# Attention and two expert layers on one core: value tiles padded with zeros, roots taken in groups, input rows added by transfers, earlier loads between phases, and the reciprocal on GpSimd

## The chip, the core and the metric

The kernel runs on one core of a Trainium2 chip. Its time is the device time of one execution in microseconds; the execution that the profiler recorded is one more. TensorE (PE; its weight loads are PEld) multiplies matrices into PSUM, VectorE is DVE, ScalarE is ACT, GpSimd is POOL, and SP only issues transfers. Each engine works through its own list of instructions in order and waits on semaphores.

## The reference

Two layers over 4096 tokens of width 256, all in float32, each closed by a layer norm:

```python
h = x + attention(rmsnorm(x, s1))             # 16 heads of 16, chunks of 64 tokens
h = h + moe(rmsnorm(h, s2))                   # 8 experts, top 2, capacity 1280, gelu, hidden 1024
x = layernorm(x + h)
x = layernorm(x + ffn(x))                     # layernorm inside, 8 experts, top 2, silu(g) * u, capacity 1280
```

The attention is linear. With phi(y) = elu(y) + 1, q and k rotated (rope) and then put through phi, v plain and g a sigmoid gate, each chunk first adds itself to the state and then reads it:

```python
S = S + einsum('bhtd,bhte->bhde', kc, vc)
Z = Z + kc.sum(axis=2)
num = einsum('bhtd,bhde->bhte', qc, S)
den = einsum('bhtd,bhd->bht', qc, Z)[..., None] + 1e-06
out = gc * (num / den)
```

The experts take the first 1280 tokens that chose them; their outputs, scaled by the gates, are added to the token's row.

## The kernel before

There are six phases, each a block in which every engine has its list, and between which all engines meet: `attention_phase`, `routing_phase`, `expert_phase` (E1), `between_phase` (norm, second router, second routing), `expert_phase` (E2), `final_phase` (norm and store).

**Attention** goes over 32 tiles of 128 tokens. `run_tiles` calls `step(t, at)` on every engine; in it `at(d)` is tile t + d, so one step holds work on several tiles: tile t+1 is projected and rotated, tile t updates the state and reads it, tile t-1 is gated and goes through the output projection, tile t-2 is normed and stored. The order on each engine is the order of the `if` blocks in its `step`. The pieces that the change touches, by the profile's lines:

- The values (L409, DVE) are written to `va`, 128 rows; the two chunks of the tile are its upper and lower 64 rows, and `add_chunk` (L459, PE) multiplies the 64 rows of one chunk with those of the keys into the state `b_s`, where 8 more columns of ones give Z. Masks (L384, DVE) copy the state after each chunk. L537 multiplies it by q: the state product.
- den is the last 8 columns per half of that product plus 1e-6 (L389, DVE), `rden` its reciprocal (L392, DVE, 128x16), `gr` gate times rden (L264, POOL), `og` is num times gr (L425, DVE). L522 transposes og, L345 copies it, L544 multiplies it by Wo. The gate is tanh with an affine step (L332, L336, ACT).
- x1 is the output of attention plus the input and bias (L400, DVE, from xb, L287, POOL). X += x1 (L270, POOL) is stored as the accumulator `acc1` (SP), and the normed x1 as `xn1`.
- The two rms norms take a mean square (ACT) to the power -0.5 on POOL, one column for each tile: r1 (L295) and r2 (L283).
- Rope needs rb (L279, POOL, two halves), ra (L437) and their sum rot (L445) on DVE; then ex (L361, ACT) and phi (L406, DVE).
- In the 16 steps of `W_STEPS` ACT and POOL also split a part of the first expert's weights (L357, L300).

Ahead of the steps, DVE scales all attention weights by the norm's scale (L370, L371), ACT and DVE split them into a high and a low part (L307, L374), and `extend_weights` (L475 to L484, PE) folds Wo and the router. DVE waits for all small loads at once.

**The seams.** At the end of an expert phase GpSimd waits for its last scatter into `acc1` or `acc2` (`pool.wait_ge(s_ys, ...)`), then all engines meet. The next phase loads the accumulator into X in eight groups of four tiles (L1108, L1256) and works group by group. To fill TensorE's time, `keep_busy` (L1061) runs matmuls whose result nobody reads: 46 at the end of E1, 12 ahead of the second router, and one for each tile there.

## Time and profile before

| | us |
|---|---|
| median of 3 runs | 1609.31 |
| lowest and highest | 1609.05, 1611.48 |
| the profiled execution | 1607.13 |
| its span | 1605.2 |

| engine | busy, share of the span |
|---|---|
| PE | 93% |
| PEld | 89% |
| DVE | 64% |
| POOL | 49% |
| ACT | 45% |

The span runs from the first to the last instruction recorded. Attention ends at about 253 us, the first routing at 288, E1 at 777, the second norm and routing at 852, and E2 at 1571. The row PEclk of the profile shows TensorE's granted clock in tenths of full speed.

### The profile page before, as it was taken

The page shows a single profiled execution, that of the slowest core. Times are in us where ns is not written, and L with a number is a line of the kernel's source. Part 1 is how long each engine was busy: PE and PEld are TensorE (multiplying, and loading weights), DVE is VectorE, ACT ScalarE, POOL GpSimd, SP SyncE. Part 2 cuts the span into 40 slices and gives each one's busy share as a digit, 9 for nine tenths or more (in the row PEclk, how much of TensorE's full clock was granted, in tenths as well). Part 3 has the DMA queues.
Part 4 walks back from the last instruction along what each step waited for, and adds up shares of the span by engine and source line. Part 5 has one row for each costly group of instructions (what it writes and reads, how often), then busy time and mean ns, then how long its engine had stood idle before and what let it go on. Part 6 is the DMA issues. An engine that isn't in the chain of part 4 may idle for free. (4 is left out here: it accounts for less than half of the span.)

```text
span 1605.2 us, 36263 instructions
## 1 busy us (share of the span) xinstructions
PE 1491.0 (93%) x11777; PEld 1435.2 (89%) x11777; DVE 1025.9 (64%) x2891; ACT 729.9 (45%) x1737; POOL 790.6 (49%) x799
## 2 busy tenths in 40 slices
PE   5999995799999999999967999999999999999990
PEld 4877774799999999999866999999999999999990
DVE  4888887567667667667374556565655656565553
ACT  3666554445455455555353434344343434343324
POOL 3899981456666566664322443444344344334420
PEclk9999996799999999999976999999999999999995
DMA  7111110333433343352412141323132132312216
GB/s 245 38 37 41 41 41 20 112 95 46 100 92 49 95 96 54 87 128 37 144 80 102 27 115 30 105 33 108 30 75 66 30 105 33 112 27 31 35 15 216
DMA packets 63829, 119.28 MB, mean 74 GB/s; under 512 B 14481, under 2 KB 52881, under 8 KB 61585
## 3 DMA queue, kind: packets, MB, share of 16 engines
q0 software_dynamic: 35840, 42.38, 16.1%
q1 hardware_dynamic: 27920, 76.07, 13.1%
q8 instruction: 32, 0.52, 0.1%
q14 instruction: 37, 0.30, 0.1%
HBM read 79.71 MB, written 38.71 MB: 74 GB/s over the span
## 5 line engine op out<-in xcount | busy, mean ns | idle before, releaser
L841 POOL DMA_INDIRECT acc<-E_ysb,IDX x160 | 258.4, 1615 | 133.8 <-ACT E_ysb L931 65.3
L836 POOL DMA_INDIRECT E_mg<-meta,IDX x160 | 151.0, 944 | 336.1 <-DVE E_gate L952 310.2
L968 DVE TENSOR_TENSOR E_hraw<-E_sg,bank 128x256 f32<-128x256 f32 x320 | 134.6, 421 | 283.3 <-ACT E_sg L904 283.3
L1021 PE MATMUL bank<-E_xT,ws 128*128 128x256 f32 x960 | 271.5, 283 | 5.0 <-DVE E_xT L943 5.0
L1022 PE MATMUL bank<-E_xT,ws 128*128 128x256 f32 x960 | 271.0, 282 | 0.0
L1023 PE MATMUL bank<-E_xT,ws 128*128 128x256 f32 x960 | 270.7, 282 | 0.0
L979 DVE TENSOR_TENSOR E_hT<-E_hraw,E_hT 128x256 fp32r<-128x256 f32 x640 | 259.3, 415 | 0.0
L975 DVE CAST E_hT<-E_hraw 128x256 fp32r<-128x256 f32 x640 | 201.1, 314 | 60.0 <-ACT E_hraw L907 52.9
L904 ACT ACTIVATE E_sg<-bank 128x256 f32<-128x256 f32 x320 | 121.4, 384 | 253.1 <-PE bank L1023 251.4
L1021 PEld LDWEIGHTS bank<-E_xT,ws 128*128 128x128 f32 x960 | 182.5, 190 | 5.8 <-issue 5.8
L1021 PE MATMUL bank<-ws,E_hT 128*128 128x256 f32 x640 | 183.7, 287 | 0.0
L1022 PEld LDWEIGHTS bank<-E_xT,ws 128*128 128x128 f32 x960 | 182.6, 190 | 0.0
L1023 PEld LDWEIGHTS bank<-E_xT,ws 128*128 128x128 f32 x960 | 182.4, 190 | 0.0
L1023 PE MATMUL bank<-ws,E_hT 128*128 128x256 f32 x640 | 180.1, 281 | 0.0
L1022 PE MATMUL bank<-ws,E_hT 128*128 128x256 f32 x640 | 180.0, 281 | 0.0
L1021 PE MATMUL bank<-E_xT,ws1b 128*128 128x256 f32 x640 | 179.5, 280 | 0.0
L1022 PE MATMUL bank<-E_xT,ws1b 128*128 128x256 f32 x640 | 179.5, 280 | 0.0
L1023 PE MATMUL bank<-E_xT,ws1b 128*128 128x256 f32 x640 | 179.4, 280 | 0.0
L907 ACT ACTIVATE E_hraw<-bank,E_b 128x256 f32<-128x256 f32 x320 | 141.7, 474 | 48.6 <-PE bank L1023 40.6
L831 POOL DMA_INDIRECT E_xg<-acc,IDX x80 | 80.6, 1007 | 146.8 <-ACT E_xgn L886 101.8
L467 PE MATMUL bank<-A_wsp,A_xT 128*128 128x512 f32 (+2 forms) x576 | 119.7, 344 | 4.4 <-DVE A_xT L433 4.4
L831 POOL DMA_INDIRECT E_xg<-xn,IDX x80 | 82.1, 1026 | 83.6 <-PE bank L1014 39.0
(201 smaller groups left out, 3990.4 us busy)
## 6 DMA issues: line engine op xcount, KB each, us to landing
wraw<-in_w_ffn SPq DMA_DIRECT2D x8, 3072.0 KB, 10.4
wraw<-in_w_moe SPq DMA_DIRECT2D x8, 2048.0 KB, 8.0
X<-acc SPq DMA_DIRECT2D x16, 512.0 KB, 6.8
xn<-A_xn SPq DMA_DIRECT2D x32, 128.0 KB, 1.7
acc<-X SPq DMA_DIRECT2D x32, 128.0 KB, 1.8
acc<-X SPq DMA_DIRECT2D x8, 512.0 KB, 2.6
out<-C_xo SPq DMA_DIRECT2D x8, 512.0 KB, 2.8
X<-in_x SPq DMA_DIRECT2D x3, 1024.0 KB, 11.4
```

The lines of the kernel that those rows point to most:

```text
L467: ins = nc.tensor.matmul(out, xT[:, n % 2, a, k, :], wsp[:, b, k, cols], start=(k == 0 and m == 0), stop=(k == KD - 1 and m == 2))
L831: nc.gpsimd.indirect_dma_start(out=xg[:, j, :], out_offset=None, in_=row_dram, in_offset=at_slots(u, j)).then_inc(s_gx, 16)
L836: nc.gpsimd.indirect_dma_start(out=mg[:, j, :], out_offset=None, in_=meta_dram, in_offset=at_slots(u, j)).then_inc(s_gm, 16)
L841: nc.gpsimd.indirect_dma_start(out=acc_dram, out_offset=at_slots(u, j), in_=ysb[:, j, :], in_offset=None, compute_op=ALU.add).then_inc(s_y ...
L904: nc.scalar.activation(sg[:, f % RING, :], ps[:, 0:UW], ACT.Silu).then_inc(s_sg, 1)
L907: nc.scalar.activation(hraw[:, f % RING, :], ps[:, 0:UW], ACT.Gelu, bias=b1[:, bass.ds(e * NF + f, 1)]).then_inc(s_sg, 1)
L968: V.tensor_tensor(hraw[:, f % RING, :], sg[:, f % RING, :], bank[f % RING][:, UW:2 * UW], ALU.mult).then_inc(s_hm, 1)
L975: V.tensor_copy(hT[:, 0, f, :], hraw[:, f % RING, :]).then_inc(s_hh, 1)
L979: V.tensor_tensor(hT[:, 1, f, :], hraw[:, f % RING, :], hT[:, 0, f, :].bitcast(F32), ALU.subtract).then_inc(s_hl, 1)
L1021: nc.tensor.matmul(out, wh, mh, start=first, stop=False)
L1022: nc.tensor.matmul(out, wh, ml, start=False, stop=False)
L1023: return nc.tensor.matmul(out, wl, mh, start=False, stop=last)
```

## The change

It has these parts:

1. **Values padded with zeros.** `vf` (DVE) takes the values; ACT copies each chunk's 64 rows into a tile `vz` of its own, whose other 64 rows are zero. `add_chunk` multiplies all 128 rows.
2. **Reciprocal on GpSimd.** rden = den to the power -1, 128x16, on POOL. DVE forms `ng` = (tanh + 1) x num, POOL og = ng x rden; the factor 0.5 goes into Wo ahead of the steps. The affine step on ACT is gone.
3. **Grouped roots.** r1 is taken for 1, 3 and then 4 tiles at once, r2 for 2; the xn and logit rows follow in pairs. ACT sums the squares of the input five tiles ahead instead of three.
4. **Input rows by transfers.** SP stores x1 into acc1; POOL issues four transfers of 8 tiles (`add_plain`) that add X to it. E1 waits for them.
5. **Start.** Weights come in two halves, scaled while they are split; the first tile of X has its own transfer; TensorE runs 16 matmuls on zeros first, and the folding of Wo stands later.
6. **Early rows.** SP loads the first two groups of X inside the expert phase, when all scatters but the last unit's have landed (those tiles aren't in the last unit), and the other six in the next phase after the last has. GpSimd no longer waits, and blocks end without its drain. The fillers go from 46 to 26 and from 12 to 4.

The core of the diff:

```diff
+            pool.wait_ge(loads, 16 * 4)
+            nc.gpsimd.tensor_scalar(wo[:, :, 0:D], wo[:, :, 0:D], 0.5, 0.0, ALU.mult, ALU.add).then_inc(s_half, 1)
 ...
                 if (n := at(-1)) is not None:
+                    pool.wait_ge(s_den, n + 1)
+                    after(pool, s_og, n)
+                    nc.gpsimd.tensor_tensor(rden[:, :, :], den[:, :, :], less1[:, :].unsqueeze(2).to_broadcast([P, KD, HPH]),
+                                            ALU.pow).then_inc(s_rden, 1)
                     pool.wait_ge(s_rden, n + 1)
-                    pool.wait_ge(s_g, n + 1)
-                    nc.gpsimd.tensor_tensor(by_head(gr[:, n % 2, :]), by_head(gt[:, n % 2, :]),
+                    pool.wait_ge(s_ng, n + 1)
+                    nc.gpsimd.tensor_tensor(by_head(og[:, n % 2, :]), by_head(ng[:, :]),
                                             rden[:, :, :].rearrange("p k h -> p (k h)").unsqueeze(2).to_broadcast([P, H, DK]),
-                                            ALU.mult).then_inc(s_gr, 1)
-                if (n := at(-2)) is not None:
-                    nc.gpsimd.tensor_tensor(X[:, n, :], X[:, n, :], x1[:, n % 2, 0:D], ALU.add).then_inc(s_xacc, 1)
+                                            ALU.mult).then_inc(s_og, 1)
 ...
+                if t in (11, 19, 27):
+                    add_plain(nc, pool, io, X, kept, t // 8 - 1)
+def add_plain(nc, pool, io, X, kept, g):
+    t = slice(g * 8, (g + 1) * 8)
+    for b in range(2):
+        pool.wait_ge(kept[f"x1{b}"], 16 * (g + 1) * 4)
+    nc.gpsimd.dma_start(by_partition(io["acc1"])[:, t, :], X[:, t, :], accum_op=ALU.add).then_inc(kept["plus"], 16)
 ...
+                    for c in range(2):
+                        rows = slice(c * CHUNK, (c + 1) * CHUNK)
+                        nc.scalar.activation(vz[rows, n % 2, c, :, 0:P], vf[rows, :, :], ACT.Copy).then_inc(s_vz, 1)
 ...
-                    dve.wait_ge(s_den, n + 1)
-                    V.reciprocal(rden[:, :, :], den[:, :, :]).then_inc(s_rden, 1)
+                    dve.wait_ge(s_th, n + 1)
+                    V.scalar_tensor_tensor(out=ng[:, :].rearrange("p (k c) -> p k c", k=KD), in0=gt[:, n % 2, :].rearrange("p (k c) -> p k c", k=KD),
+                                           scalar=1.0, in1=num_ps[:, :, 0:P], op0=ALU.add, op1=ALU.mult).then_inc(s_ng, 1)
 ...
-                    ins = nc.tensor.matmul(s_ps[:, k, :], phi[rows, n % 2, D + k * P:D + (k + 1) * P],
-                                           va[rows, n % 2, k, :], start=False, stop=True, skip_group_check=True)
+                    ins = nc.tensor.matmul(s_ps[:, k, :], phi[:, n % 2, D + k * P:D + (k + 1) * P],
+                                           vz[:, n % 2, c, k, :], start=False, stop=True, skip_group_check=True)
 ...
+            sp.wait_ge(s_ys, 16 * UT * (UNITS - 1))
+            for g in range(HEAD):
+                t = slice(g * G, (g + 1) * G)
+                sp.dma_start(X[:, t, :], by_partition(acc_dram)[:, t, :]).then_inc(s_head[g], 16)
 ...
-            pool.wait_ge(s_ys, 16 * UT * UNITS)
-                keep_busy(nc, bank[7], ws[0], 46)
+                keep_busy(nc, bank[7], ws[0], 26)
 ...
-            for g in range(GROUPS):
+            sp.wait_ge(s_ys, 16 * UT * UNITS)
+            for g in range(HEAD, GROUPS):
 ...
-            keep_busy(nc, bank[7], ws0, 12)
+            keep_busy(nc, bank[7], ws0, 4)
```

GpSimd's list in one attention step with expert weights, before (A_r from A_ssq is a root, ws a part of the weights):

```order
L264 TENSOR_TENSOR A_gr<-A_gt,A_rden 128x256
L270 TENSOR_TENSOR X<-X,A_x 128x256
L279 TENSOR_TENSOR A_rb<-A_qk,A_rope 128x32x8 x2
L283 TENSOR_TENSOR A_r<-A_ssq,A_mhalf 128x1
L287 TENSOR_TENSOR A_xb<-X,A_bo 128x256
L291 TENSOR_TENSOR A_xb<-A_lx,A_bor 128x8
L295 TENSOR_TENSOR A_r<-A_ssq,A_mhalf 128x1
L300 TENSOR_TENSOR ws<-wraw,ws 128x256
```

and now:

```order
L288 TENSOR_TENSOR A_rden<-A_den,A_less 128x16
L293 TENSOR_TENSOR A_og<-A_ng,A_rden 128x256
L302 TENSOR_TENSOR A_rb<-A_qk,A_rope 128x32x8 x2
L306 TENSOR_TENSOR A_r<-A_ssq,A_mhalf 128x2
L310 TENSOR_TENSOR A_xb<-X,A_bo 128x256
L314 TENSOR_TENSOR A_xb<-A_lx,A_bor 128x8
L325 TENSOR_TENSOR ws<-wraw,ws 128x256
```

The addition into X is gone, a power of 16 elements has come ahead of og, and r2 comes for two tiles in every second step.

VectorE's list in one attention step, before, from og on:

```order
L425 TENSOR_TENSOR A_og<-bank,A_gr 128x256
L384 TENSOR_TENSOR A_sm<-bank,cst 128x272
L433 TENSOR_TENSOR A_xT<-bank,A_xT 128x256
L437 TENSOR_TENSOR A_ra<-A_qk,A_rope 128x512
L384 TENSOR_TENSOR A_sm<-bank,cst 128x272
L445 SCALAR_TENSOR_TENSOR A_rot<-A_ra,A_rb 128x512
L389 TENSOR_SCALAR A_den<-bank 128x16
L392 RECIPROCAL A_rden<-A_den 128x16
L400 TENSOR_TENSOR A_x<-bank,A_xb 128x264
L406 SCALAR_TENSOR_TENSOR A_phi<-A_ex,A_rot 128x512
L409 SCALAR_TENSOR_TENSOR A_va<-bank,A_r,A_bqkvg 128x2x128
L414 SCALAR_TENSOR_TENSOR A_gt<-bank,A_r,A_bqkvg 128x256
```

and now, from the first mask on:

```order
L446 TENSOR_TENSOR A_sm<-bank,cst 128x272
L423 TENSOR_TENSOR A_xT<-bank,A_xT 128x256
L446 TENSOR_TENSOR A_sm<-bank,cst 128x272
L496 TENSOR_TENSOR A_ra<-A_qk,A_rope 128x512
L501 SCALAR_TENSOR_TENSOR A_rot<-A_ra,A_rb 128x512
L505 SCALAR_TENSOR_TENSOR A_vf<-bank,A_r,A_bqkvg 128x256
L457 TENSOR_SCALAR A_den<-bank 128x16
L460 SCALAR_TENSOR_TENSOR A_ng<-A_gt,bank 128x256
L469 TENSOR_TENSOR x<-bank,A_xb 128x264
L475 SCALAR_TENSOR_TENSOR A_phi<-A_ex,A_rot 128x512
L479 SCALAR_TENSOR_TENSOR A_gt<-bank,A_r,A_bqkvg 128x256
L485 SCALAR_TENSOR_TENSOR A_qk<-bank,A_r,A_bqkvg 128x512
```

The reciprocal is gone, ng stands behind den, ra behind the second mask, and the values behind rot.

TensorE's list at the start, from tile 0's value projection on, before:

```order
L467 MATMUL bank<-A_wsp,A_xT 128x256 x6
L467 MATMUL bank<-A_wsp,A_xT 128x264 x6
L475 MATMUL bank<-cst,A_wo 128x128 x4
L481 MATMUL bank<-A_wqkvg,A_woT 128x8 x4
L484 MATMUL bank<-A_wqkvg,A_bob 128x8 x2
L467 MATMUL bank<-A_wsp,A_xT 128x512 x6
L501 MATMUL bank<-cst,X 128x128 x2
L507 MATMUL bank<-cst,A_phi 128x128 x2
L457 MATMUL bank<-A_zeros 128x272
L459 MATMUL bank<-A_va,A_phi 128x136 x2
```

and now:

```order
L528 MATMUL bank<-A_wsp,A_xT 128x264 x6
L543 MATMUL bank<-cst,A_wo 128x128 x4
L528 MATMUL bank<-A_wsp,A_xT 128x512 x6
L536 MATMUL bank<-cst,X 128x128 x2
L574 MATMUL bank<-cst,A_phi 128x128 x2
L518 MATMUL bank<-A_zeros 128x272
L520 MATMUL bank<-A_vz,A_phi 128x136 x2
L528 MATMUL bank<-A_wsp,A_xT 128x256 x6
L520 MATMUL bank<-A_vz,A_phi 128x136 x2
L528 MATMUL bank<-A_wsp,A_xT 128x264 x6
L551 MATMUL bank<-A_wrs,A_woT 128x8 x4
L554 MATMUL bank<-A_wrs,A_bob 128x8 x2
```

The products with the transposed Wo and the bias (L481 and L484 before, L551 and L554 now; the projections are L467 before, L528 now) have moved from ahead of tile 1's projection to behind tile 0's state update.

## Rows read from the trace of the kernel before

**Rows 1.** busy time by engine in two windows: attention, second expert phase (columns as named)
```profile
core 0: us, PE busy (x) PEld busy (x) DVE busy (x) ACT busy (x) POOL busy (x), PEclk, DMA share, GB/s
200.00:240.00 40.00, 39.92 (x258) 31.74 (x256) 33.91 (x76) 22.55 (x71) 33.02 (x46) 1.00 0.11 37
866.00:1566.00 700.00, 700.00 (x5906) 700.00 (x5906) 409.13 (x1144) 271.15 (x582) 272.99 (x230) 1.00 0.26 59
```

**Rows 2.** timeline of TensorE's weight loads in one attention step (start us, us, what)
```profile
212.30 1.34 PEld L467 LDWEIGHTS bank<-A_wsp,A_xT 128*128 128x128 f32 x6
214.44 0.53 PEld L459 LDWEIGHTS bank<-A_va,A_phi 64*128 64x128 f32 x4 [0.17 <-issue]
215.10 0.78 PEld L467 LDWEIGHTS bank<-A_wsp,A_xT 128*128 128x128 f32 x6
216.01 0.53 PEld L459 LDWEIGHTS bank<-A_va,A_phi 64*128 64x128 f32 x4
216.67 0.20 PEld L522 LDWEIGHTS bank<-cst,A_og 128*128 128x128 f32 x2
219.17 1.34 PEld L467 LDWEIGHTS bank<-A_wsp,A_xT 128*128 128x128 f32 x6
```

**Rows 3.** GpSimd's instructions by form, attention, 180 to 235 us
```profile
L279 POOL TENSOR_TENSOR A_rb<-A_qk,A_rope 128x256 f32<-128x256 f32 x16 | 11.3, 729 | 6.9 <-DVE A_qk L420 6.9
L270 POOL TENSOR_TENSOR X<-X,A_x 128x256 f32<-128x256 f32 x9 | 9.4, 1039 | 1.0 <-DVE A_x L400 0.5
L287 POOL TENSOR_TENSOR A_xb<-X,A_bo 128x256 f32<-128x256 f32 x8 | 9.3, 1162 | 0.0
L283 POOL TENSOR_TENSOR A_r<-A_ssq,A_mhalf 128x1 f32<-128x1 f32 x8 | 8.0, 1004 | 0.0
L264 POOL TENSOR_TENSOR A_gr<-A_gt,A_rden 128x256 f32<-128x256 f32 x8 | 5.0, 622 | 0.1
L295 POOL TENSOR_TENSOR A_r<-A_ssq,A_mhalf 128x1 f32<-128x1 f32 x7 | 3.8, 548 | 0.0
L291 POOL TENSOR_TENSOR A_xb<-A_lx,A_bor 128x8 f32<-128x8 f32 x8 | 1.6, 200 | 0.0
```

**Rows 4.** two of VectorE's by form, same stretch
```profile
L400 DVE TENSOR_TENSOR A_x<-bank,A_xb 128x264 f32<-128x264 f32 x8 | 3.5, 433 | 4.8 <-PE bank L544 4.8
L392 DVE RECIPROCAL A_rden<-A_den 128x16 f32<-128x16 f32 x8 | 2.0, 254 | 0.3
```

**Rows 5.** timeline of the start, VectorE and TensorE
```profile
14.09 0.48 DVE L377 TENSOR_SCALAR A_bob<-cst,A_bcol 128x128 f32<-128x128 f32 x2 [1.34 <-DMA A_bcol<-in_bcol]
...
31.33 0.69 PE L537 MATMUL bank<-A_sm,A_qT 128*64 128x136 f32 x8
```

**Rows 6.** timeline between attention and the first routing
```profile
252.49 0.29 ACT L351 ACTIVATE LG<-A_x,A_r 128x8 f32<-128x8 f32 x1
...
255.40 0.43 DVE L636 TENSOR_TENSOR LG<-LG,rbias 128x256 f32<-128x256 f32 x1 [4.74 <-PEq L116]
```

**Rows 7.** timeline between the first experts and the second routing
```profile
772.00 10.60 PE L1061 MATMUL bank<-ws 128*128 128x512 f32 x46
...
775.79 1.55 POOL L841 DMA_INDIRECT acc<-E_ysb,IDX  x1 [0.30 <-issue]
...
783.71 4.04 SPq L1108 DMA_DIRECT2D X<-acc  x8
...
785.58 4.58 PE L1061 MATMUL bank<-ws 128*128 128x512 f32 x12
790.00 0.38 PE L1210 MATMUL bank<-cst,X 128*128 128x128 f32 x2
```

**Rows 8.** timeline between the second experts and the final norm
```profile
1577.41 3.95 SPq L1256 DMA_DIRECT2D X<-acc  x8
1581.22 1.41 DVE L1298 BATCH_NORM_STATS2 C_st<-X 128x6 f32<-128x256 f32 x4 [18.41 <-DMA X<-acc]
...
1587.15 2.06 ACT L1274 ACTIVATE C_xo<-X,C_nb,C_rs 128x256 f32<-128x256 f32 x4
```

More of the change, by code:

```diff
@@ L36 @@
 UT = UW // P
+G = 4
+GROUPS = NT // G
+HEAD = (UPE - 1) * UW // (G * P)
 SC = E * TILES_E
@@ L93, in after @@
         eng.sem_inc(passed, 1)
-LEAD = 3
+LEAD = 5
 LAG = 2
+R1_GROUPS = [(0, 1), (1, 4)] + [(a, a + 4) for a in range(4, NT, 4)]
+X_SPANS = [(0, 1), (1, 4), (4, 8), (8, 16), (16, 24), (24, 32)]
 WX = 4 * D + E
@@ L104 @@
 W_STEPS = range(6, 22)
+WARM = 16
 WCHUNK = 4 * HID // len(W_STEPS)
@@ L219, in _ @@
             sp.dma_start(bo[:, :], io["bo"].partition_broadcast(P)).then_inc(loads, 16)
-            sp.dma_start(bcol[:, :], io["bcol"]).then_inc(loads, 16)
-            for g in range(1, 5):
+            sp.dma_start(cst[:, C_ID + P:C_N], io["consts"][:, C_ID + P:C_N]).then_inc(l_cst, 16)
+            for g in range(2, len(X_SPANS)):
                 rows_in(g)
@@ L304, in _, with high, turned @@
         def _(act):
-            for k in range(KD):
-                act.wait_ge(s_w, 2 * k + 2)
-                nc.scalar.activation(wsp[:, 0, k, :], wqkvg[:, k, :], ACT.Copy).then_inc(s_wh, 1)
+            def high(k, part):
+                nc.scalar.activation(wsp[:, 0, k, part], wqkvg[:, k, part], ACT.Copy, scale=cols[:, k:k + 1]).then_inc(s_wh, 1)
+            def turned(n):
+                act.wait_ge(s_tx, n + 1)
+                after(act, s_pjg, n - 1)
+                after(act, s_xl, n - 1)
+                nc.scalar.activation(xT[:, n % 2, 0, :, :], tx_ps, ACT.Copy).then_inc(s_xT, 1)
+            act.wait_ge(l_cols, 16)
+            act.wait_ge(l_wa, 16)
+            for k in range(KD):
+                high(k, half_a)
+            turned(0)
+            act.wait_ge(l_wb, 32)
+            for k in range(KD):
+                high(k, slice(2 * D, 4 * D))
+            act.wait_ge(s_wrs, KD)
+            for k in range(KD):
+                nc.scalar.activation(wsp[:, 0, k, 4 * D:WX], wrs[:, k, :], ACT.Copy).then_inc(s_wh, 1)
             def step(t, at):
@@ L450, in _ @@
         def _(pe):
-            pe.wait_ge(early, 16 * 5)
-            pe.wait_ge(s_cst, 4)
+            pe.wait_ge(s_cst, 1)
+            for _ in range(WARM):
+                nc.tensor.matmul(b_to[:, 0:KD * SW], zeros[:, 0:P], zeros[:, :], start=True, stop=True)
             def add_chunk(n, c):
-                rows = slice(c * CHUNK, (c + 1) * CHUNK)
                 if n % TPB == 0 and c == 0:
@@ L458, in add_chunk, with project, turn, turn_weights @@
                 for k in range(KD):
-                    ins = nc.tensor.matmul(s_ps[:, k, :], phi[rows, n % 2, D + k * P:D + (k + 1) * P],
-                                           va[rows, n % 2, k, :], start=False, stop=True, skip_group_check=True)
+                    ins = nc.tensor.matmul(s_ps[:, k, :], phi[:, n % 2, D + k * P:D + (k + 1) * P],
+                                           vz[:, n % 2, c, k, :], start=False, stop=True, skip_group_check=True)
                 ins.then_inc(s_sa, 1)
-            def project(n, out, cols):
+            def project(n, out, part):
                 for k in range(KD):
                     for m, (a, b) in enumerate(((0, 0), (0, 1), (1, 0))):
-                        ins = nc.tensor.matmul(out, xT[:, n % 2, a, k, :], wsp[:, b, k, cols],
+                        ins = nc.tensor.matmul(out, xT[:, n % 2, a, k, :], wsp[:, b, k, part],
                                                start=(k == 0 and m == 0), stop=(k == KD - 1 and m == 2))
                 return ins
-            def extend_weights():
-                pe.wait_ge(loads, 16 * 5)
+            def turn(n):
+                loaded(pe, n)
+                after(pe, s_xl, n)
+                for k in range(KD):
+                    ins = nc.tensor.transpose(tx_ps[:, k, :], X[:, n, k * P:(k + 1) * P], ident)
+                ins.then_inc(s_tx, 1)
+            def turn_weights():
+                pe.wait_ge(s_half, 1)
                 for m in range(KD):
@@ L495, in step @@
                     after(pe, s_qk, n)
-                    project(n, b_p0[:, :], slice(0, 2 * D)).then_inc(s_pj0, 1)
-                if (n := at(2)) is not None:
-                    loaded(pe, n)
-                    after(pe, s_xl, n)
-                    for k in range(KD):
-                        ins = nc.tensor.transpose(tx_ps[:, k, :], X[:, n, k * P:(k + 1) * P], ident)
-                    ins.then_inc(s_tx, 1)
+                    project(n, b_p0[:, :], half_a).then_inc(s_pj0, 1)
+                if (n := at(2)) is not None and n:
+                    turn(n)
                 if (n := at(0)) is not None:
@@ L846, in free_rows @@
                 pool.wait_ge(s_xgn if glu else s_tg, n * UT if glu else n)
+            if kept:
+                for b in range(2):
+                    pool.wait_ge(kept[f"xn{b}"], 16 * NT // 2)
             x_rows(0)
@@ L853, in _ @@
             meta_rows(1)
+            if kept:
+                pool.wait_ge(kept["plus"], 16 * NT // 8)
             for u in range(UNITS):
```

290 lines of the change are left out of this document (159 added, 131 removed).

## The prediction

> **What bounds the kernel now.** I read the stages first, as busy time in windows. The reader should see two kinds of stretch. In the second expert phase TensorE's weight loads fill 700.00 of 700 us at a granted clock of 1.00 [rows 1]; the change leaves the work inside both expert phases alone, so nothing moves there. In the attention phase, 40 us hold 39.92 us of matmuls but 31.74 us of weight loads, beside 33.91 us of VectorE and 33.02 us of GpSimd [rows 1]: three engines near the limit at once.
>
> So I read one attention step engine by engine. A step takes 219.17 - 212.30 = 6.87 us on TensorE, in which no wait for another engine stands, only gaps: 0.17 us ahead of the first state update (L459), 0.13 us behind it (215.10 - 214.97), 0.13 us ahead of the second (216.01 - 215.88) and 0.13 us behind it (216.67 - 216.54) [rows 2]. These are the places where the array goes from 128 rows to 64 and back. TensorE bounds the step. GpSimd idles there only for qk, 6.9 us in 8 steps, which is 0.86 us a step [rows 3]; VectorE idles 4.8 us for the output projection in 8 steps [rows 4], 0.6 us a step. A step shorter by more than about 0.9 us would meet one of the two.
>
> Last come the seams between phases: times at which one phase's last instruction and the next one's first stand apart [rows 5 to 8].
>
> **The state update on 128 rows.** Values go into a tile whose other half is zero, so L459's matmuls no longer use half of the array. The loads stay as many and as wide (4 in 0.53 us [rows 2]), so all there is to win is the four gaps, 0.56 us; they will not vanish wholly. I take 0.38 us a step, bounds 0 and 0.56. The price is two ScalarE copies of 64 partitions instead of the gate's affine step (L336), on an engine that waits several times a step for others: hidden, nothing. VectorE loses the reciprocal (0.254 us [rows 4]), and its og gives way to ng, as wide. Over 30 full steps: 30 x 0.38 = 11.4 us, if GpSimd keeps up.
>
> The Trainium skill, "TensorE: Matmul & The Clock Gate", Part 3, speaks against this edit: it says that a weight load runs under a matmul in flight only where the two use different row groups, an overlap which full-height matmuls give up. The trace shows no such overlap ahead of L459, but the gap of 0.17 us [rows 2]. By that rule alone this term would be 0 or a small loss; it is one of the rivals below.
>
> **GpSimd's step.** Removed: X += x1 (1.04 us), half of the r2 powers (1.00 each, beside a VectorE instruction), three of four r1 powers (0.55). gr (0.62) becomes og, of the same size. Added: rden as a power of 16 elements [rows 3]. What stays is 0.62 + 2 x 0.73 + 0.50 + 1.16 + 0.20 + about 0.15 = 4.1 us, and in the 16 steps that also split expert weights one more 256-wide instruction, 0.62: 4.7 us.
>
> What the power costs no row shows, since each power in this trace has one element. Below: 0.55 us, plus 15 elements at the rate of a plain operation, (0.622 - 0.200) / 248 = 0.0017 us each: 0.57 us. Above: a plain one-element operation is 0.19 us, so one power is 0.55 - 0.19 = 0.36 us more, and if each element pays that, it is 0.19 + 16 x 0.36 = 5.95 us. Which of the two the 0.36 us is, a preparation or a price per element, decides the case. I take 1.6 us, nearer to the one-element row than to the upper end. Then GpSimd needs 5.7 us a step, and 6.3 us in the steps with weights: under the 6.49 us of TensorE, by little. The Trainium skill, "GPSIMD Engine Reference", section 3.1, calls the operation a software loop over the elements in which the body is paid for each, and 4.1 advises against this engine for elementwise work. By it the upper bound is the likelier end; it is the first rival.
>
> The power adds a wait too, for den. og is wanted by the transpose L522, which stands 4.37 us into a step (216.67 - 212.30 [rows 2]), so for it a power of 3 us would still be in time. Behind the power on GpSimd are queued og and then rb, for which VectorE's rot waits. Before, X += x1 stood in that place and GpSimd then idled for qk, 1.04 + 0.86 us [rows 3]; only a power over 1.9 us makes rb late.
>
> **X plus x1 by transfers.** SP stores x1 instead of X, and four accumulating transfers of 1 MB add X later. A scatter of 128 rows takes GpSimd 1.55 us to issue [rows 7]; four issues, at most 6 us, in the idle time of the step. 0, bound 3 us. No wait is late by them: the only one who needs the sum is the first scatter, over 30 us on.
>
> **The start.** Before, VectorE passes its wait for all small loads at 14.09, and the first state product of tile 0 runs at 31.33 [rows 5]. In between lie the scaling of the weights and the folded router weights, which stood ahead of the second projection on TensorE. After, scaling is folded into the two splits, the weights come in halves, the roots of the first tiles are there early, and the folding stands behind the gate projection. What is loaded up to the last of the small loads falls from 3.1 to 2.7 MB, so they are in by about 14.09 x 2.7 / 3.1 = 12.3. An estimate of the chain from there, each instruction about 0.7 us and GpSimd's pair 1.5 [rows 3]: qk to 13.1, rb to 15, rot, ex and phi to 17.8, then gt, qk, two masks with TensorE between them, ra, rot, ex and the copies of the second round to about 24, the product at 24.5. That is 6.8 us earlier; the 16 warming matmuls on zeros may hold the first transpose, so I take 6.5, bounds 3 and 9.
>
> **The end of attention.** Before: the last router row at 252.49, the routing's first instruction at 255.40 [rows 6], 2.9 us, of which I take half as the wait for the last stores, which goes: 1.5 us. The last tile pays the power instead of 0.25 us, and the xn and logit rows of two tiles instead of one (about 0.8 us): -2.2 us. Sum -0.7.
>
> **First experts to the second routing.** Before, the last scatter is issued by 777.34, and everybody waits for it to land: the next phase begins at 783.71, and loads X, and TensorE turns the first tile at 790.00 after twelve filling matmuls [rows 7]. After, only SP waits for it; the phase opens at about 778.3, when GpSimd has issued and TensorE has run 26 instead of 46 fillers (46 took 10.60 us, so 26 end at 778.0 [rows 7]), and two of eight groups of X are there, loaded during the last unit. TensorE needs 785.58 - 783.71 = 1.87 us for the fold [rows 7] and 0.9 for four fillers: first turn at 781.1, which is 8.9 us earlier. When the scatter has landed no row shows; it is before 783.71, and I take 0.6 us before. The third group is there 3.8 us later (as a first group, 1581.22 - 1577.41 [rows 8]), at 786.9, about when the first eight tiles are turned. I take 8.5, bounds 5 and 10.
>
> **Second experts to the final norm.** Here ScalarE bounds the end, group behind group. The third group can't be loaded before the scatter has landed, again taken as 0.6 us before the opening, 1576.8, so it lands at 1580.6 and reaches ScalarE at 1583.0, with 2.4 us for its moments and root; before, the second group's rows started at 1587.15 [rows 8], and they come just ahead of it in the queue. So 4.1 us, bounds 3 and 7.
>
> **The sum.** 11.4 + 6.5 - 0.7 + 8.5 + 4.1 = 29.8 us. The profiled execution took 1607.1 us, its span 1605.2; it becomes 1577.3. The median of the runs is 2.2 us above it: 1579.
>
> **Rivals.**
> - *The power pays per element.* GpSimd becomes the bound of the attention step. With a power of p us the steps change by 14 x (p + 4.1 - 6.87) + 16 x (p + 4.7 - 6.87) = 30 p - 73.5 us, against 20 - p us won elsewhere. It decides from p = 3.0 us: there the change is worth nothing. At 4 us it is slower by 30 us (1640), at 5.95 by 91 us (1700). For it: 0.36 us for one element is much for mere preparation. Against it: a loop over independent elements may overlap them.
> - *Between the two*, 2.2 to 3.0 us: GpSimd eats the steps' gain and part of the rest, 1585 to 1609.
> - *The steps do not get shorter*, since the gaps stay, or VectorE's order (second mask, ra, rot, vf, den, ng, x1) closes a loop of the old length. All else holds: 1607.1 - 18.4, and with the median's offset 1591. For it: VectorE idles in only 0.9 us of a step, and TensorE's second update waits for its mask.
> - *The change does not do what it says* in the seams (the next phase still opens when the scatter has landed): 13 us less gain, 1592. SP is then the one that opens late; its order has the wait inside the next phase, so this is small.
>
> **Chances.** Forecast 0.48; the power per element, slower, 0.30; between 0.12; steps not shorter 0.07; seams 0.03. Within 0.2% (3.2 us, about what a measurement of this kernel tells from none) lies a sliver of the middle case: 0.04. Faster is 0.48 + 0.07 + 0.03 + 0.08 = 0.66, slower 0.30. The range reaches from 1570 (all terms at their good ends but one) to 1655 (a power of 4.5 us), which leaves out the highest powers; the forecast's own range is 1570 to 1592.
>
> **What the profile of the changed kernel would show.** The mean of the power of 16 elements on GpSimd: near 1.6 us, or several. The step on TensorE at 6.5 us, no gap beside the state updates, and no wait for og. GpSimd idle at rb for qk; if it never idles there, the first rival holds. The first state product near 24.5, TensorE's first turn of the second routing under 8 us behind the last expert matmul's 772, and the final phase opening under 6 us behind the last scatter's issue. I am wrong if the attention phase is longer than before.

## The result, and the profile after

The changed kernel takes 1618.2 us (median of 5 runs, 1617.6 to 1620.5), the kernel before 1609.3 us in runs on the same chip. The ratio is 1.0057, 95% interval 1.0041 to 1.0072: slower by 0.6%, where 1579 us were forecast. Its profiled execution took 1619.0 us, with a span of 1617.2 us, 12.0 more than before.

Where the 12.0 us come from, stretch by stretch. The attention steps are counted from the first instruction that writes the denominators (`A_den`) to the last, 31 intervals; "last scatter" is the start of its issue.

| Stretch | before | after | change | forecast |
|---|---|---|---|---|
| start to the first denominators | 32.1 | 26.8 | -5.3 | -6.5 |
| 31 attention steps | 213.5 | 243.5 | +30.0 | -11.4 |
| last denominators to routing | 9.9 | 11.1 | +1.2 | +0.7 |
| E1, last scatter to the first turned tile | 14.2 | 5.5 | -8.7 | -8.5 |
| E2, last scatter to the last output rows | 32.5 | 24.5 | -8.0 | -4.1 |
| all the rest: both routings, both expert phases, the last stores | | | +2.8 | 0 |

The four stretches at the start, the end of attention and the seams together won 20.8 us where 18.4 were forecast. The steps lost 41 us against the forecast. The windows show on which engine (columns: window, its length, then busy time with count for PE, PEld, DVE, ACT, POOL, then TensorE's granted clock, DMA share and GB/s):

```profile
60.00:200.00 140.00, 115.96 (x733) 93.73 (x732) 98.76 (x201) 77.01 (x249) 131.94 (x132) 0.96 0.19 49
200.00:240.00 40.00, 35.47 (x237) 29.13 (x238) 31.20 (x66) 22.32 (x74) 39.04 (x37) 1.00 0.09 31
```

Against [rows 1], TensorE falls from 39.92 to 35.47 us of 40, and GpSimd rises from 33.02 to 39.04: it hardly rests. Its instructions by form in the stretch of [rows 3] (busy us and mean ns of one, then the idle time ahead):

```profile
L288 POOL TENSOR_TENSOR A_rden<-A_den,A_less 128x16 f32<-128x16 f32 x7 | 21.1, 3009 | 0.5 <-DVE A_den L457 0.5
L302 POOL TENSOR_TENSOR A_rb<-A_qk,A_rope 128x256 f32<-128x256 f32 x14 | 11.7, 859 | 0.0
L310 POOL TENSOR_TENSOR A_xb<-X,A_bo 128x256 f32<-128x256 f32 x8 | 6.7, 837 | 0.0
L293 POOL TENSOR_TENSOR A_og<-A_ng,A_rden 128x256 f32<-128x256 f32 x7 | 4.8, 686 | 0.6
L306 POOL TENSOR_TENSOR A_r<-A_ssq,A_mhalf 128x2 f32<-128x2 f32 x4 | 2.8, 690 | 0.0
```

The 16-element power takes 3.0 us, not 1.6, and rb no longer waits for qk: the sign that the prediction gave for its first rival. By size it stands at the upper end of the prediction's middle case (2.2 to 3.0 us, 1585 to 1609); the kernel came out 9 us above that case. TensorE's loads show both the promised gain and the new wait:

```profile
200.01 0.20 PEld L574 LDWEIGHTS bank<-cst,A_phi 128*128 128x128 f32 x2 [1.20 <-DVE A_phi L475]
200.18 0.53 PEld L520 LDWEIGHTS bank<-A_vz,A_phi 128*128 128x128 f32 x4
200.64 0.78 PEld L528 LDWEIGHTS bank<-A_wsp,A_xT 128*128 128x128 f32 x6
201.52 0.53 PEld L520 LDWEIGHTS bank<-A_vz,A_phi 128*128 128x128 f32 x4
203.93 0.20 PEld L592 LDWEIGHTS bank<-cst,A_og 128*128 128x128 f32 x2 [1.88 <-POOL A_og L293]
```

The gaps of [rows 2] around the first state update are gone (200.18 follows 200.01, and 200.64 follows 200.18, without a pause); ahead of the second 0.10 us is left (201.42 to 201.52) of 0.13. But TensorE stands 1.20 us for phi and 1.88 us for og, which GpSimd hands over late. At the seams:

```profile
26.02 0.69 PE L611 MATMUL bank<-A_sm,A_qT 128*64 128x136 f32 x8 [1.79 <-issue]
...
280.23 0.28 ACT L388 ACTIVATE LG<-x,A_r 128x8 f32<-128x8 f32 x1
281.31 0.43 DVE L710 TENSOR_TENSOR LG<-LG,rbias 128x256 f32<-128x256 f32 x1 [3.44 <-PEq L130]
...
802.54 1.55 POOL L920 DMA_INDIRECT acc<-ysb,IDX  x1 [0.30 <-issue]
806.44 2.81 SPq L1188 DMA_DIRECT2D X<-acc  x6
808.08 0.38 PE L1290 MATMUL bank<-cst,X 128*128 128x128 f32 x2
...
1589.30 1.55 POOL L920 DMA_INDIRECT acc<-ysb,IDX  x1 [0.30 <-issue]
1592.82 2.97 SPq L1337 DMA_DIRECT2D X<-acc  x6
1596.83 1.41 DVE L1379 BATCH_NORM_STATS2 C_st<-X 128x6 f32<-128x256 f32 x4 [5.73 <-DMA X<-acc]
```

The first state product comes 5.3 us earlier than in [rows 5]. The wait of 2.9 us in [rows 6] is 1.1 us. The loads that need the scatter start 3.5 to 3.9 us behind the scatter's issue; before, 7.9 us in [rows 7] (783.71 - 775.79) and 8.0 at the last seam.

### The profile page after: what moved, and what is told of

The parts are those of the page before. It is cut to its first block and busy times, and to the rows that moved or that the text cites. A ratio compares the mean times of both kernels' runs of the same rounds, so it can differ in the third digit from the quotient of the medians.

```text
span 1617.2 us, 36347 instructions
## 1 busy us (share of the span) xinstructions
PE 1487.6 (92%) x11781; PEld 1436.5 (89%) x11781; DVE 1021.5 (63%) x2861; ACT 740.7 (46%) x1773; POOL 834.3 (52%) x767
## 5 line engine op out<-in xcount | busy, mean ns | idle before, releaser
L920 POOL DMA_INDIRECT acc<-ysb,IDX x160 | 258.2, 1614 | 134.7 <-ACT ysb L1014 66.0
L1106 PEld LDWEIGHTS bank<-ws,E_hT 128*128 128x128 f32 x640 | 121.0, 189 | 0.0
## 6 DMA issues: line engine op xcount, KB each, us to landing
wraw<-in_w_ffn SPq DMA_DIRECT2D x8, 3072.0 KB, 10.5
```

Of the source, the lines that this page charges most:

```text
L920: nc.gpsimd.indirect_dma_start(out=acc_dram, out_offset=at_slots(u, j), in_=ysb[:, j, :], in_offset=None, compute_op=ALU.add).then_inc(s_y ...
L1106: return nc.tensor.matmul(out, wl, mh, start=False, stop=last)
```

## The experiments

Each run's steps are the same 31 intervals, counted in its profiled execution. The ratios go by runs of the kernel before that were made beside each kernel; their medians were 1609.3 to 1611.9 us. In one table:

| Kernel | median us | ratio to before, 95% | 31 steps | us a step |
|---|---|---|---|---|
| before | 1609.3 | | 213.5 | 6.89 |
| changed | 1618.2 | 1.0041 to 1.0072 | 243.5 | 7.85 |
| e3: before + power | 1667.2 | 1.0315 to 1.0380 | 267.9 | 8.64 |
| e1: reciprocal on VectorE | 1590.5 | 0.9841 to 0.9903 | 218.4 | 7.04 |
| e2: half of it as a power | 1582.2 | 0.9792 to 0.9854 | 207.1 | 6.68 |
| e9: e1 + power nobody reads | 1580.0 | 0.9797 to 0.9829 | 206.7 | 6.67 |
| e14: e1, og behind qk | 1593.2 | 0.9867 to 0.9909 | 217.5 | 7.02 |
| e6: e1, roots tile by tile | 1589.4 | 0.9854 to 0.9896 | 215.9 | 6.96 |
| e15: e14 and e6, and final order | 1576.2 | 0.9763 to 0.9812 | 203.8 | 6.57 |
| e13: e2, roots tile by tile | 1587.8 | 0.9844 to 0.9877 | 212.8 | 6.86 |
| e5: changed, roots tile by tile | 1613.6 | 1.0017 to 1.0037 | 239.5 | 7.73 |
| e10: e2, updates on 64 rows | 1589.9 | 0.9865 to 0.9907 | 216.8 | 6.99 |
| e11: e2 with the drain | 1586.6 | 0.9843 to 0.9876 | 205.9 | 6.64 |
| e17: e2, no early rows | 1588.8 | 0.9838 to 0.9893 | 207.0 | 6.68 |
| e16: e14, no warming | 1592.3 | 0.9855 to 0.9910 | 217.7 | 7.02 |

Run e4, further down, is no version of the kernel and has no row. Kernels e2, e11 and e17 have the same steps, which shows how far 31 steps repeat: 205.9 to 207.1.

### What a power costs

> This kernel computes nothing of the reference: on 128 partitions GpSimd runs a power and a multiplication three times each at 1, 2, 4, 8, 16, 32 and 64 elements, nothing beside it, and then VectorE runs reciprocals of the same sizes. If a power is paid per element (theory), the means lie on a line: from the changed kernel's trace (548 ns for one element, 690 for two, 1007 for four, about 2.9 us for 16) near 0.39 + 0.156 us per element, so 5.4 us at 32 and 10.4 us at 64, while the multiplications stay near 0.2 to 0.3 us. If the 2.9 us were contention with the kernel's other engines (rival), 16 elements would take here what a preparation and a plain rate give, under 1 us.

Rows of four short windows, each holding one size:

```profile
L49 POOL TENSOR_TENSOR y<-x,h 128x1 f32<-128x1 f32 x3 | 1.7, 558 | 0.2
L49 POOL TENSOR_TENSOR y<-x,h 128x1 f32<-128x1 f32 x3 | 0.6, 190 | 0.2
...
L49 POOL TENSOR_TENSOR y<-x,h 128x16 f32<-128x16 f32 x3 | 8.7, 2896 | 0.2
...
L49 POOL TENSOR_TENSOR y<-x,h 128x64 f32<-128x64 f32 x1 | 10.5, 10527 | 0.1
```

The first row is the power of one element, the second the multiplication; the last two are powers. The power takes 558, 699, 1007, 1636, 2896, 5418 and 10,527 ns for 1 to 64 elements: a straight line of 0.38 us plus 0.158 us an element ((10.527 - 0.558) / 63). The theory holds; the rival falls, since nothing ran beside it. VectorE's reciprocal of 16 elements took 0.255 us here.

```diff
 # e3: before, in front of gr on GpSimd; the reciprocal on VectorE goes
+pool.wait_ge(s_den, n + 1)
+nc.gpsimd.tensor_tensor(rden, den, less1 (broadcast), ALU.pow).then_inc(s_rden, 1)
```

> The kernel before with one edit: the reciprocals as a 16-element power on GpSimd, ahead of gr. Theory (GpSimd's step is the sum of its instructions): it had 6.87 - 0.86 = 6.0 us of work a step, and 2.9 to 3.2 more make about 9.0, so 30 steps grow by 60 to 70 us: 1670 to 1680. Rival (only the wait for the denominators counts, and GpSimd's idle time takes most of the power): under 30 us longer, below 1640.

It is slower by 3.5%, and the rival falls: the steps grew by 54.4 us, from 213.5 to 267.9, a little under the theory's 60 to 70. The step is 8.64 us, not 9.0. The sum had taken the durations of the kernel before; with GpSimd as the bound some of its instructions are shorter:

```profile
L263 POOL TENSOR_TENSOR A_rden<-A_den,A_less 128x16 f32<-128x16 f32 x16 | 49.2, 3075 | 1.2 <-DVE A_den L394 1.2
L274 POOL TENSOR_TENSOR X<-X,A_x 128x256 f32<-128x256 f32 x16 | 11.7, 728 | 0.0
L287 POOL TENSOR_TENSOR A_r<-A_ssq,A_mhalf 128x1 f32<-128x1 f32 x16 | 9.6, 603 | 0.0
```

X += x1 is 0.73 instead of 1.04 us, and r2's power 0.60 instead of 1.00 [rows 3], while each half of rb is 0.92 instead of 0.73. The likely reason, which no run tests, is that they lie elsewhere beside VectorE's instructions. So in the kernel before the power alone costs 54 us of steps. The changed kernel's steps grew by 30 only; it had also taken X += x1 off GpSimd and grouped the roots.

### The power undone, and at the price that was assumed

```diff
 # e1: DVE, behind den
-(GpSimd) nc.gpsimd.tensor_tensor(rden, den, less1, ALU.pow).then_inc(s_rden, 1)
+V.reciprocal(rden[:, :, :], den[:, :, :]).then_inc(s_rden, 1)
 # e2: both engines, half each
+nc.gpsimd.tensor_tensor(rden[:, 0, :], den[:, 0, :], less1, ALU.pow).then_inc(s_rden, 1)
+V.reciprocal(rden[:, 1, :], den[:, 1, :]).then_inc(s_rdv, 1)
```

> The changed kernel with the reciprocal back on VectorE, all else kept. Theory: the 16-element power of 2.9 to 3.3 us alone makes the attention steps longer. GpSimd's step falls to 4.1 us (4.7 with weights), TensorE bounds it again, and the 31 intervals between the first and the last denominator take 202 to 214 us instead of 243.5; median 1578 (if the 128-row updates save 0.38 us a step) to 1589 (if they save nothing). Rival: the roots in pairs and the normalized rows of two tiles at a time, which tie ScalarE to GpSimd, make a good part of it: then the attention keeps over 225 us and the median is 1600 or more.

> The changed kernel, with the reciprocals of one half (8 elements) as a power on GpSimd and those of the other half on VectorE. By 0.39 + 0.156 us per element the power takes 1.64 us, the value that the prediction assumed for all 16, so this run measures whether the rest of the prediction's sum holds at that price: 1579 if its account of the step is right (GpSimd 5.7 us a step, 6.3 with weights, hidden under TensorE). Rival: a power of any such length is late for the two instructions behind it on GpSimd (the output copy and rb, for which VectorE waits), because it waits for the denominators first; then this is slower than the kernel with the reciprocal on VectorE by 10 us or more.

With the reciprocal on VectorE the kernel is 1.3% faster than the kernel before, so the power is the cause of the sign. But its steps, at 7.04 us, are longer than before, outside the 202 to 214 us that the theory gave and also far from its rival's 225. With half of the reciprocals, GpSimd's power is

```profile
L288 POOL TENSOR_TENSOR A_rden<-A_den,A_less 128x8 f32<-128x8 f32 x21 | 35.0, 1668 | 4.2 <-DVE A_den L458 4.2
```

1.67 us, the value assumed for all 16, and the median is 1582.2 against the 1579 forecast for that price. That the version with more work on GpSimd is faster by 8 us needed an explanation. VectorE's phi gives the lead, first e1, then e2 (60 to 200 us):

```profile
L473 DVE SCALAR_TENSOR_TENSOR A_phi<-A_ex,A_rot 128x512 f32<-128x512 f32 x20 | 20.6, 1031 | 0.0
```

```profile
L478 DVE SCALAR_TENSOR_TENSOR A_phi<-A_ex,A_rot 128x512 f32<-128x512 f32 x21 | 14.4, 684 | 0.0
```

The same instruction takes 1.03 us in the one and 0.68 in the other, with no wait ahead of it in either. The timeline of e1 says what lies beside it:

```profile
148.22 0.62 POOL L289 TENSOR_TENSOR A_og<-A_ng,A_rden 128x256 f32<-128x256 f32 x1
```

```profile
147.72 0.36 DVE L458 SCALAR_TENSOR_TENSOR A_ng<-A_gt,bank 128x256 f32<-128x256 f32 x1
148.00 0.42 DVE L467 TENSOR_TENSOR x<-bank,A_xb 128x264 f32<-128x264 f32 x1
148.33 1.05 DVE L473 SCALAR_TENSOR_TENSOR A_phi<-A_ex,A_rot 128x512 f32<-128x512 f32 x1
```

GpSimd's og starts as soon as ng is there, and so runs into phi. In e2 the power is beside phi, and og comes beside qk, which reads PSUM and keeps its 0.74 us (e2, GpSimd, then VectorE):

```profile
149.04 1.62 POOL L288 TENSOR_TENSOR A_rden<-A_den,A_less 128x8 f32<-128x8 f32 x1
150.74 0.62 POOL L294 TENSOR_TENSOR A_og<-A_ng,A_rden 128x256 f32<-128x256 f32 x1
```

```profile
149.38 0.68 DVE L478 SCALAR_TENSOR_TENSOR A_phi<-A_ex,A_rot 128x512 f32<-128x512 f32 x1
150.38 0.74 DVE L488 SCALAR_TENSOR_TENSOR A_qk<-bank,A_r,A_bqkvg 128x512 f32<-128x512 f32 x1
```

### Two locks on the step

A lock here is a wait or a slow instruction that holds the step's length by itself, so that removing another one shows nothing.

```diff
 # e9: all 16 reciprocals on VectorE; on GpSimd in the same place
+nc.gpsimd.tensor_tensor(unused[:, :], den[:, 0, :], less1, ALU.pow).then_inc(s_rden, 1)
```

> All 16 reciprocals on VectorE; GpSimd also takes a power of 8 elements at the same place, whose result nobody reads. The kernel with half of the reciprocals on GpSimd ran 8.2 us faster than the one with all on VectorE (1582.2 against 1590.5; 31 steps in 207.1 against 218.4 us), though it gives GpSimd 1.67 us more a step and takes only 0.05 us from VectorE's reciprocal. Theory: GpSimd's elementwise instructions slow VectorE's longest ones where the two lie side by side (phi 1.03 instead of 0.68 us), and the power, which does not, moves them away from phi. Then this kernel keeps phi near 0.68 us and takes 1582 to 1585. Rival: the 0.05 us of the shorter reciprocal stand on VectorE's chain, and with what hangs on them make the difference; then this is 1588 to 1592 with phi at 1.0 us.

The unused power alone brings 218.4 down to 206.7 us, with phi at 681 ns: the theory holds, the rival falls. The median, 1580.0 us, is even 2 us under its range. GpSimd's extra 1.67 us worked as a delay of og. The next question was whether the delay can be had without the work.

```diff
 # e14: e1, GpSimd, ahead of og of tile t-1
+if (n := at(1)) is not None:
+    pool.wait_ge(s_qk, n + 1)
```

> All 16 reciprocals on VectorE, no power on GpSimd, and one wait more: GpSimd starts og only when VectorE has written qk of two tiles on. Theory: it is og (0.62 us) beside phi, an instruction that reads and writes SBUF alone, that stretched phi from 0.68 to 1.03 us in the plain version; the power helped only because it kept GpSimd's og away from phi. With og behind qk, phi is 0.68 us, 31 steps take 206 to 208 us, and the median is 1578 to 1583. Rival: the later og is late for TensorE's transposes (the wait moves to them), or the next instructions in line, rb and xb, now lie beside ra and rot longer: 31 steps stay over 212 us and the median over 1585.

A miss: the steps stay at 7.02 us. Phi is mostly short now (758 ns on average), but VectorE waits for something else, and ScalarE for the root of a pair (e14, VectorE and ScalarE by form, 60 to 200 us):

```profile
L475 DVE SCALAR_TENSOR_TENSOR A_phi<-A_ex,A_rot 128x512 f32<-128x512 f32 x20 | 15.2, 758 | 5.9 <-ACT A_ex L396 5.9
```

```profile
L385 ACT ACTIVATE xn<-x,A_r 128x256 f32<-128x256 f32 x20 | 10.0, 501 | 13.4 <-POOL A_r L304 13.4
```

Every second step ScalarE waits for r2 of two tiles and then normalizes both, ahead of the next ex; in the steps whose phi starts at 134.12, 149.19 and 163.51, VectorE has stood 0.66 to 0.68 us for ex; between them it does not. The step's length alternates with it, 6.4 and 7.3 us once the steps with weights are over. Undoing the pairs alone (e6), and both together (e15):

```diff
 # e6 and e15: GpSimd, ScalarE, SP
-if (n := at(-2)) is not None and n % 2:    # r2, xn, logits and the stores of n - 1 and n
+if (n := at(-2)) is not None:              # of n
 # e15 also, in the final phase: scales(1) and normal(1) ahead of the wait for group 2
```

For e15, then for e6:

> The same, with two more edits that lie in different stretches: roots, normalized rows and router rows tile by tile instead of in pairs, and in the final phase the rows of group 1 normalized before the wait for group 2. If the pairs cost anything besides the power of the wrong size (theory from the run that undid them: 243.5 to 239.5 us in 31 steps), the attention gets shorter by 1 to 4 us; rival: with GpSimd no longer the bound nothing, or 1 us lost by ten more powers of 0.55. The final phase: ScalarE idled 5.3 us with group 1 ready; the reorder takes 1 us off what lies behind the last scatter (28 to 27 us), at most 2.

> All 16 reciprocals on VectorE, and roots, normalized rows and router rows tile by tile instead of in pairs; og doesn't wait for qk. Theory A (pairs): the pair of normalized rows on ScalarE, which waits for the pair's root, stands ahead of the next exponential, and every second step is longer by it; undone, 31 steps take 202 to 206 us as in the version with both edits (203.8), median 1576 to 1579. Theory B (og beside phi): undoing the pairs alone leaves phi near 1.0 us and VectorE as the bound; 31 steps stay over 212 us, median over 1586. Both needed: between, 207 to 212 us.

Alone, neither helps (7.04 to 7.02 and 6.96 us a step); together they give 6.57. In e6 phi is 1063 ns: theory B was right there and theory A wrong. In e14 phi was short and the pairs held the step. Both locks have to be opened. Going from e14 to e15 takes away VectorE's wait for ex (5.9 us in 140), and it also shortens rot, from 872 to 708 ns on average, which neither theory had named. In e15 TensorE is the bound of the step again, first the window, then its loads:

```profile
60.00:200.00 140.00, 139.50 (x944) 116.14 (x943) 124.41 (x282) 97.79 (x319) 106.79 (x152) 1.00 0.21 58
```

```profile
141.21 0.53 PEld L520 LDWEIGHTS bank<-A_vz,A_phi 128*128 128x128 f32 x4
141.67 0.78 PEld L528 LDWEIGHTS bank<-A_wsp,A_xT 128*128 128x128 f32 x6
142.55 0.53 PEld L520 LDWEIGHTS bank<-A_vz,A_phi 128*128 128x128 f32 x4
143.00 0.26 PEld L592 LDWEIGHTS bank<-cst,A_og 128*128 128x128 f32 x2
```

Its median of 1576.2 us is the best of all, 2.1% under the kernel before. The reorder in the final phase, expected to win 1 us, won 0.4 in one execution of each: last scatter to end 27.5 us instead of the 28.0 of e14. ScalarE waits 3.35 us for group 2 instead of 5.46, but then 1.55 us more for group 3, with no ready group left to fill them.

The same undoing of the pairs was tried on two more kernels, the changed one (e5) and e2 (e13):

> The changed kernel with all 16 reciprocals on GpSimd, but the second roots, the normalized rows and the router rows tile by tile instead of in pairs. Theory (GpSimd's step is the sum of its instructions): 0.55 a step instead of 0.69 in every second one, so GpSimd has 0.2 us a step more, the alternation of 9.4 and 6.9 us in the steps with weights evens out, and the sum grows by 3 to 7 us: 1621 to 1626. Rival: the pairs hold ScalarE up for the roots and GpSimd for ScalarE's weights (6.8 us of idle time in 16 steps), and the even order wins more than the 0.2 us cost: below 1615.

> Half of the reciprocals as an 8-element power on GpSimd, and roots, normalized rows and router rows tile by tile instead of in pairs: the change with the price of its power cut to the 1.6 us that the prediction took and without the pairs. If the pairs cost every kernel in which GpSimd is not the bound (theory A), 31 steps fall from 207.1 to 202 to 204 us, the prediction's 11.4 us less than 213.5, and the median to 1576 to 1579. Rival: the pairs cost only where no power stands between VectorE's denominators and og; then nothing changes, or the ten powers more (0.55 us each) put GpSimd at its limit and the steps get longer: 207 to 210 us, 1582 to 1586.

Undoing the pairs won 3.9 us of steps in the changed kernel (rival right, theory wrong), but lost 5.7 us in the kernel with half of the power, more than either expectation. There GpSimd is busy for 135.54 of 140 us, and its instructions are longer, which is put down to their lying beside VectorE's long ones, without a run of its own: the 8-element power 1907 ns instead of 1668, rb 898 instead of 748. A root now costs 601 ns for each tile, where it was 700 for two. So whether the pairs help depends on which engine is the bound, and no rule for them follows from these runs.

### The padding

```diff
 # e10: e2, add_chunk on the non-zero half of the padded tile
-phi[:, n % 2, ...], vz[:, n % 2, c, k, :]
+phi[c * CHUNK:(c + 1) * CHUNK, n % 2, ...], vz[c * CHUNK:(c + 1) * CHUNK, n % 2, c, k, :]
```

> The kernel with half of the reciprocals on GpSimd, but the state updates read 64 rows again (the padded tile stays as it is, only its non-zero half is used). Theory, the prediction's term: the gaps of 0.13 to 0.17 us at each change between 128 and 64 rows come back, 0.38 us a step, and TensorE, at 97% busy, bounds the step: 31 steps in 219 instead of 207 us, median 1594. Rival: VectorE's chain bounds the step (it idles 0.6 us in 6.7), so the gaps cost nothing to 0.1 us a step: 1582 to 1585.

31 steps take 216.8 instead of 207.1 us, 0.31 us a step, and the median is 7.7 us above e2: the theory's direction, four fifths of its size. The gap is back, and VectorE's wait for the state grows (21.6 us in 140 instead of 12.3):

```profile
200.44 0.53 PEld L523 LDWEIGHTS bank<-A_vz,A_phi 64*128 64x128 f32 x4 [0.17 <-issue]
201.09 0.77 PEld L531 LDWEIGHTS bank<-A_wsp,A_xT 128*128 128x128 f32 x6
201.99 0.53 PEld L523 LDWEIGHTS bank<-A_vz,A_phi 64*128 64x128 f32 x4
202.65 0.20 PEld L595 LDWEIGHTS bank<-cst,A_og 128*128 128x128 f32 x2
```

Four loads and the gap behind them take 0.65 us on 64 rows (201.09 - 200.44) and 0.46 us on 128 (141.67 - 141.21 in e15), though the load rows themselves read 0.53 in both.

### The seams and the start

```diff
 # e11: e2, all phases
-nc.Block(no_gpsimd_drain=True)
+nc.Block()
 # e17: e2
-HEAD = (UPE - 1) * UW // (G * P)
+HEAD = 0
```

> The kernel with half of the reciprocals on GpSimd, with the drain of GpSimd at the end of every phase back; the early loads of input rows stay. It tells apart what the two seams won, 8.7 us behind the first experts and 8.0 behind the second. Theory: the drain made every engine wait for the last scatter and some 4 us more, so it takes back 5 to 8 us at each seam, and the early loads by themselves keep 1 to 3 us: median 1592 to 1598. Rival: the early loads are what counts, since the third group of rows must wait for the scatter anyway; then the drain takes back under 3 us at a seam and the median is below 1588.

> The kernel with half of the reciprocals on GpSimd, and no early input rows: all eight groups are loaded when the scatters have landed; the drain stays away. With the drain back and the early rows kept, the seams lost 3.7 us (last scatter of the first experts to the first turn: 5.5 to 9.2) and 1.9 us (last scatter of the second experts to the end: 27.7 to 29.6). If the rest of the gain at the seams (5.0 and 6.1 us of 8.7 and 8.0) is the early rows, this kernel shows 10 to 11 us and 33 to 34 us. Rival: most of it is that only SP waits for the landing; then the early rows are worth under 2.5 us at each: below 8 and 30.

The theory for the drain was too high. The last scatter's issue to the first turned tile takes 5.5 us in e2, 9.2 with the drain and 7.6 without the early rows; the last scatter to the end of the span 27.8, 29.6 and 31.6 us. So at the first seam the drain is worth 3.7 and the early rows 2.0 us of the 8.7, at the last 1.9 and 3.9 of the 8.0. The rest, 3.0 and 2.2 us, is what neither run undoes: that only SP waits for the landing, and at the first seam also the fewer fillers (26 and 4 instead of 46 and 12). No run tells these apart, and none takes out drain and early rows together. How late the loads come that need the scatter (e11):

```profile
1554.37 1.55 POOL L923 DMA_INDIRECT acc<-ysb,IDX  x1 [0.30 <-issue]
...
1559.89 2.92 SPq L1340 DMA_DIRECT2D X<-acc  x6
```

5.5 us behind the issue with the drain, against 3.5 to 3.9 us without, and 7.9 to 8.0 in the kernel before, where GpSimd first waited for the landing and was drained after it.

```diff
 # e16: e14
-WARM = 16
+WARM = 0
```

> The same as the version with og behind qk, without the 16 warming matmuls on zeros at the start of TensorE. The prediction took 0.3 us off the start for them, and the start won 5.3 us, 1.2 less than it said. If they hold the first transpose, the first denominator comes 0.5 to 1.5 us earlier than 26.8 us. Rival: they keep the granted clock at the higher level, and without them the first projections run at the lower one: first denominator 0 to 3 us later.

The first denominators come at 28.2 us instead of 27.4, on the rival's side, but this decides nothing: in the twelve kernels that have the changed start with the warming, e14 among them, they come between 26.7 and 29.5 us, and the two medians, 1592.3 and 1593.2 us, don't differ. What the traces do show goes both ways. Without the warming the first transpose runs at 6.18 instead of 10.68 us, so the warming does hold it up. But then the first six matmuls of the projection take 2.90 us instead of 1.62. The granted clock from 15 to 27 us is 0.86 without the warming and 0.96 with it, between its two levels of 1.2 and 2.4 GHz, and 0.86 too in e13, which is warmed. In the 15 us before, TensorE was busy for 6.04 us in e16 and for 12.62 in e14. Whether the warming is worth anything stays open.

## Why the prediction was wrong

**The step that failed is the price of the power.** The prediction bounded it by 0.57 and 5.95 us and took 1.6, "nearer to the one-element row than to the upper end". It is 2.90 us alone and 3.0 to 3.2 in the kernel. The question that it named, preparation or price per element, was the right one; the answer is both: of the 0.37 us that one power costs more than one multiplication (0.56 - 0.19), 0.158 us is paid for each element and 0.21 once. No row of before could tell, since all its powers had one element. 1.6 us was a value between two mechanisms, worked out from neither. Taking half of the 0.36 us as paid per element would have given 0.37 + 16 x 0.18 = 3.3 us, with the rival as the forecast.

The Trainium skill, "GPSIMD Engine Reference", section 3.1, which the prediction named, describes the body as paid for each element. By that rule the trace agrees: 10.5 us for 64 elements.

**The rival's formula.** By 30p - 73.5 a power of 3.0 us makes the steps longer by 16.5 us; they grew by 30.0. Its busy time per step was right: 131.94 us in 16.6 steps is 7.9, against 4.7 + 3.2 = 7.9. It left out that GpSimd, now the bound, can wait too. In the steps with weights it stands for ScalarE's half of the split:

```profile
L325 POOL TENSOR_TENSOR ws<-wraw,ws 128x256 fp32r<-128x256 f32 x16 | 11.7, 730 | 6.8 <-ACT ws L394 6.8
L288 POOL TENSOR_TENSOR A_rden<-A_den,A_less 128x16 f32<-128x16 f32 x17 | 54.0, 3175 | 0.0
```

That is 6.8 us of the 13.5 missing, and the power at 3.175 instead of 3.0 us in these 17 steps is 3.0 more. Two smaller terms were wrong as well. The row ws was taken as 0.62 us and is 0.73, 1.8 us in 16 steps. The issues of the transfers, put at nothing in GpSimd's idle time, take 1.10 us at 113.72 and 0.95 at 182.52, in steps in which GpSimd no longer idles for qk. Together these come to the missing 13.5 us, but other rows moved both ways (rb and og longer, xb shorter), so this is an assignment and not a proof.

**The step of 6.5 us.** At the assumed price it was 6.68 us on average (e2), with the reciprocal on VectorE 7.04 (e1); 6.57 us came only in e15. The padding's gain was sized well, 0.31 us against 0.38. In e2 19 of the 31 intervals are 6.50 to 6.53 us long, as forecast, where most steps without weights took 6.84 to 6.87 in the kernel before. Of the 5.0 us that e2's steps lack, 3.8 lie in four intervals of 7.2 to 7.7 us, the first one and three in the steps with weights; two of these three hold the issue of a transfer, but no run takes the transfers out. What the prediction left out is the other side of GpSimd's relief: an engine that is done sooner starts its next instruction sooner, beside another of VectorE's. It did weigh VectorE's order as a loop of the old length, with 0.07, and cost the pairs only at the last tile.

**Start, -6.5 forecast, -5.3 found.** Within its bounds.

**End of attention**, +0.7 forecast, +1.2 found. The wait fell by 1.8 us, and what the last tile pays rose by 3.1 instead of 2.2 us: the power's size again.

**First seam**, 8.5 forecast, 8.7 found. Right in its steps: the phase opened at 805.2, 2.7 us behind the start of the last scatter's issue (forecast 778.3 - 775.79 = 2.5), and the first tile was turned 2.9 us later (forecast 2.8). The landing came far earlier than assumed, but the first turn doesn't need it.

**Last seam**, 4.1 forecast, 8.0 found. The term that was off is the landing, taken as 0.6 us ahead of the old opening, 7.4 us behind the issue. The loads that wait for it start 3.5 us behind, and the difference of 3.9 us is the whole error. The stretch between landing and opening was GpSimd's wait, the drain and the meeting, in a row; I had no row for it and should have kept the bounds at 3 and 9 us.

With a power of the assumed price (e2) the sum stands 3 us from the measured 1582.2, but that is partly luck, by terms that cancel: the steps won 6.4 instead of 11.4 us, the last seam about 8 instead of 4.1.

## What to carry to other kernels

A power on GpSimd is to be priced per element before it is moved there; a row with one element bounds it from one side only, and a kernel of a few lines that runs it at two sizes settles it. When GpSimd becomes free earlier, look at what of VectorE's its next instruction will lie beside, above all instructions that touch SBUF only; in e15, with the wait that holds it back, TensorE was still busy for 139.50 of 140 us. Where two edits each change little, try them together before giving either up.
